# Regrouping the attention scores through HBM and mixing the heads on four 64x64 tiles

## The reference

```python
h = tok_mixer(x)                                  # AFT-like token mixer, layernorm
q, k, v = split(layernorm(h) @ w_qkv)             # 16 heads of 64
attn = softmax(q @ k.T * 64**-0.5, axis=-1)       # (16, 257, 257)
attn = einsum('bhij,hg->bgij', attn, reattn_w)    # mixing of the heads
attn = (attn - mean over heads) * rsqrt(var over heads + 1e-3)
attn = attn * gamma[head] + beta[head]
h = h + (attn @ v) @ w_out + b_out
h = h + down(silu(gate(q8(ln(h)))) * up(q8(ln(h))))   # quantised feed-forward, inner width 1024
```

## Time and profile before

| | |
|---|---|
| median of three runs | 876.7 us |
| profiled execution, its own time | 874.84 us |
| span in the profile | 873.1 us |
| granted TensorE clock, mean | 0.935 |
| loop iterations, from transpose L498 to the next | 93.4 to 96.4 us |

### The profile page before, as it was taken

One profiled execution on the slowest core, in us unless ns is written; L12 is line 12 of the kernel. 1 busy time (PEld: TensorE's weight loads), 2 busy tenths in 40 slices (PEclk: granted clock), 3 DMA queues, 4 the chain that ended last, 5 costly groups with the idle time before them and its releaser, 6 DMA issues.

```text
span 873.1 us, 14228 instructions
## 1 busy us (share of the span) xinstructions
PE 732.1 (84%) x4514; PEld 527.8 (60%) x4514; DVE 642.9 (74%) x1442; ACT 435.2 (50%) x1198; POOL 179.6 (21%) x367
## 2 busy tenths in 40 slices
PE   1769688989998999898998999899998899788754
PEld 0446466757675777666775767477766677456521
DVE  1596758688958896888768885889688886868444
ACT  0103637563657364745747265836575574747210
POOL 0308124012310233013301231023301330013000
PEclk9959799989999999989998999899999999899877
DMA  8300410050003200230004000311023000500000
GB/s 330 129 1 0 172 46 2 17 175 9 31 1 129 72 30 0 85 107 12 24 28 164 6 30 0 128 64 36 0 73 119 13 1 28 166 7 7 1 12 0
DMA packets 25414, 49.26 MB, mean 56 GB/s; under 512 B 2715, under 2 KB 6052, under 8 KB 24740
## 3 DMA queue, kind: packets, MB, share of 16 engines
q1 hardware_dynamic: 24340, 45.34, 15.4%
q10 hardware_dynamic: 1040, 3.49, 1.0%
HBM read 13.16 MB, written 2.11 MB: 17 GB/s over the span
## 4 chain that ended last, share of the span: by engine, by line
PE 37%; issue 26%; DVE 16%; ACT 8%; POOL 8%; DMA 4%; POOLq 1%; SPq 0%; ACTq 0%; DVEq 0%
PE small L535 5%; PE big L535 5%; PE small L686 5%; PE big L552 5%; DMA pg<-pst 4%; PE big L618 4%; DVE pst L1186 3%; DVE mx L1193 2%; ACT pst L918 2%; PE big L716 2%; PE small L641 2%; PE small L671 2%; ACT ot L1007 2%; DVE var L1221 1%; POOL nww L1569 1%
## 5 line engine op out<-in xcount | busy, mean ns | idle before, releaser
L918 ACT ACTIVATE pst<-big,nb 128x256 f32<-128x256 f32 x256 | 117.7, 473 | 46.9 <-DVE nb L1196 24.5
L618 PEld LDWEIGHTS big<-w_mix,pg 128*128 128x128 f32 x1024 | 122.5, 194 | 25.9 <-DVE an L1265 18.3
L618 PE MATMUL big<-w_mix,pg 128*128 128x128 f32 x1024 | 126.3, 279 | 7.9 <-DVE an L1265 7.9
L1193 DVE TENSOR_REDUCE mx<-big 128x4 f32<-128x1024 f32 x64 | 78.2, 1222 | 26.2 <-PE big L552 25.7
L552 PE MATMUL big<-qk_t 64*128 64x256 f32 x512 | 72.6, 402 | 20.1 <-ACT qk_t L901 20.1
L939 ACT ACTIVATE sqb<-big 128x1024 f32<-128x1024 f32 x64 | 64.8, 1014 | 42.9 <-PE big L618 42.9
L1221 DVE TENSOR_REDUCE var<-sqb 128x64 f32<-128x1024 f32 x64 | 77.6, 1213 | 9.1 <-ACT sqb L939 9.1
L1265 DVE TENSOR_TENSOR an<-big,rstd 128x1024 f32<-128x1024 f32 x64 | 78.4, 1225 | 2.7 <-DVE rstd L1252 0.2
L1186 DVE TENSOR_SCALAR pst<-pst,rr 128x256 f32<-128x256 f32 x256 | 72.8, 350 | 0.0
L552 PEld LDWEIGHTS big<-qk_t 64*128 64x128 f32 x512 | 44.2, 186 | 45.6 <-ACT qk_t L901 27.9
L535 PE MATMUL small<-xnt,w_qkv 128*128 128x256 f32 x256 | 65.5, 400 | 0.0
(11 more groups left out here) (200 smaller groups left out, 1233.5 us busy)
## 6 DMA issues: line engine op xcount, KB each, us to landing
pg<-pst SPq DMA_DIRECT2D x128, 256.0 KB
w_qkv<-in_w_qkv SPq DMA_DIRECT2D x1, 3072.0 KB
xt<-in_x_t SPq DMA_DIRECT2D x8, 256.0 KB, 2.9
xr<-in_x_tok SPq DMA_DIRECT2D x8, 256.0 KB, 2.7
out<-h SPq DMA_DIRECT2D x16, 128.0 KB
an<-in_gate_t ACTq DMA_DIRECT2D x1, 1024.0 KB, 8.5
an<-in_up_t ACTq DMA_DIRECT2D x1, 1024.0 KB, 10.8
an<-in_down_t ACTq DMA_DIRECT2D x1, 1024.0 KB, 13.3
```

The source lines that it names most:

```text
L618: last = mm(mix_place(n)[:, i * P:(i + 1) * P], pg[:, hf * (IB // 2) + i, it * T + jt * P:it * T + (jt + 1) * P], w_mix[:], start=True, st ...
L918: last = A(pst[:, g % 2, h % GH, it, :], big[p % 2][:, (j * TT + it) * T:(j * TT + it + 1) * T], ACT.Exp, bias=nb[:, h, it:it + 1], scale= ...
L1193: V.reduce_max(mx[:, hs, :], big[p % 2][:, :].rearrange("p (h t l) -> p h t l", h=2, t=TT), AX)\
```

## The change

The exponentials are no longer normalised. The row sums are written behind the exponentials of a head (columns 512 and 513 of a `pst` row of 520), and each head goes by one DMA into a scratch tensor `turned` in HBM, indexed (k, head, ib, 514 floats), as soon as the sums of its pair are there. When all 16 writes have landed, two DMAs read all of it into `pg`, one for each half of the blocks `ib`, each over all 128 partitions; a partition is now k * 16 + head. DVE takes the reciprocals of the gathered sums (`row_scales`, two instructions of 128x16), and POOL multiplies the constant mixing weights by them (`scale_weights`, four instructions of 128x512, into the free first slot of `pst`). The mixing uses these weights as the moving operand, in 64x64 tiles: 30 matmuls instead of 8 in a group. The class column, its exponential and the sum are now made for each pair, not for each two pairs. The order of tokens is now made by multiplying with a permutation matrix instead of the identity where `xn` and `pck` are turned (so as matmuls, not transposes), and the copies that permuted are plain.

```diff
-    return n // 4, n // 2 % 2, n % 2
+    return n // 4, n % 2, n // 2 % 2
...
-        pst = sb("pst", [P, 2, GH, TT, T])
+        pst = sb("pst", [P, 2, GH, PW])
+        w_rows = pst[:, 0, :, :].rearrange("p j m -> p (j m)")[:, 0:TT * IB * QH * H]\
+            .rearrange("p (t i x) -> p t i x", t=TT, i=IB)
...
+        turned = nc.dram_tensor("turned", (QG, H, IB, SUM + TT), F32, kind="Internal").ap()
...
+                if not is_(b, 0):
+                    for hf in range(2):
+                        sp.wait_ge(s_pg[hf], 16 * b)
+                for p in pairs:
+                    sp.wait_ge(dve_s.sem, dve_s.at(b, ("tot", p)))
+                    for h in (2 * p, 2 * p + 1):
+                        sp.dma_start(turned[:, h, :, :], pst[:, h // GH % 2, h % GH, 0:SUM + TT])\
+                            .then_inc(s_sh[p // 2 % 2][p % 2], 16)
+
+            def gather(b):
+                if is_(b, 0):
+                    sp.wait_ge(setup_pe.sem, setup_pe.at(0, "z"))
+                else:
+                    sp.wait_ge(pe_r.sem, pe_r.at(b - 1, ("r", NMIX - 1)))
+                for s in s_sh[0] + s_sh[1]:
+                    sp.wait_ge(s, 16 * 2 * (NGRP // 2) * (b + 1))
+                for hf in range(2):
+                    ibs = slice(hf * (IB // 2), (hf + 1) * (IB // 2))
+                    sp.dma_start(pg[:, ibs, 0:SUM + TT], turned[:, :, ibs, :].rearrange("q h i m -> (q h) i m"))\
+                        .then_inc(s_pg[hf], 16)
...
-                        last = nc.tensor.transpose(bank[2][:, c * T + tt * P:c * T + (tt + 1) * P],
-                                                   xn[:, tt, c * P:(c + 1) * P], ident[:])
+                        last = mm(bank[2][:, c * T + tt * P:c * T + (tt + 1) * P],
+                                  xn[:, tt, c * P:(c + 1) * P], to_place[:], start=True, stop=True)
...
+                if jt == 0:
+                    if it == 0:
+                        pe.wait_ge(s_pg[hf], 16 * (b + 1))
+                    pe.wait_ge(pool_w.sem, pool_w.at(b, (it, hf)))
                 for i in range(IB // 2):
-                    last = mm(mix_place(n)[:, i * P:(i + 1) * P],
-                              pg[:, hf * (IB // 2) + i, it * T + jt * P:it * T + (jt + 1) * P], w_mix[:],
-                              start=True, stop=True)
+                    ib = hf * (IB // 2) + i
+
+                    for half in ((0, P),) if i == 0 else ((0, 64), (64, P)):
+                        j = slice(it * T + jt * P + half[0], it * T + jt * P + half[1])
+                        for k_hi in range(2):
+                            rows = slice(k_hi * 64, k_hi * 64 + 64)
+                            last = mm(mix_place(n)[half[0]:half[1], k_hi * 512 + i * 64:k_hi * 512 + (i + 1) * 64],
+                                      pg[rows, ib, j], w_rows[rows, it, ib, :], start=True, stop=True)
...
-                A(permuted(xnt[:].rearrange("p c l -> p (c l)")),
-                  bank[2][:, :].rearrange("p (t i k) -> p t i k", i=IB, k=QG), ACT.Copy).then_inc(act_a.sem, 1)
+                A(xnt[:], bank[2][:, :].rearrange("p (c l) -> p c l", c=MC), ACT.Copy).then_inc(act_a.sem, 1)
...
-                    normalise(g, 0)
...
+            def row_scales(b, hf):
+                dve.wait_ge(s_pg[hf], 16 * (b + 1))
+                if not is_(b, 0):
+                    dve.wait_ge(pool_w.sem, pool_w.at(b - 1, (TT - 1, hf)))
+                ibs = slice(hf * (IB // 2), (hf + 1) * (IB // 2))
+                V.reciprocal(rg[:, :, ibs], pg[:, ibs, SUM:SUM + TT].rearrange("p i t -> p t i")).then_inc(dve_w.sem, 1)
...
-                ffn_x(b, ff, P, 1, (dve_o.sem, dve_o.at(b, ("h3", 1))), lambda: ffn_out(b, ff, P, 0))
+                ffn_stats(b, ff, P, 1, (dve_o.sem, dve_o.at(b, ("h3", 1))))
+                if do_scores:
+                    row_scales(b + 1, 0)
+                ffn_norm(b, ff, P, 1)
+                ffn_quant(b, ff, P, 1)
+                ffn_out(b, ff, P, 0)
+                if do_scores:
+                    row_scales(b + 1, 1)
...
+            def scale_weights(b):
+                for hf in range(2):
+                    pool.wait_ge(dve_w.sem, dve_w.at(b, hf))
+                    for it in range(TT):
+                        ibs = slice(hf * (IB // 2), (hf + 1) * (IB // 2))
+                        G.tensor_tensor(w_rows[:, it, ibs, :], w_mix[:].unsqueeze(1).to_broadcast([P, IB // 2, QH * H]),
+                                        rg[:, it, ibs].unsqueeze(2).to_broadcast([P, IB // 2, QH * H]), ALU.mult)\
+                            .then_inc(pool_w.sem, 1)
...
                 power(b, ff["pool"], ff["dve"], ve_f, rs_f, P, slice(1, 2), ("ve", 1))
+                if do_scores:
+                    scale_weights(b + 1)
```

More of the change, by code:

```diff
@@ L77, in group, with place_of @@
 def group(n):
-    return n // 4, n // 2 % 2, n % 2
[L82 to L90, removed]
+    return n // 4, n % 2, n // 2 % 2
+def place_of(token):
+    half, k_hi, i, k_lo = token // 64, token // 32 % 2, token // QH % (IB // 2), token % QH
+    return k_hi * 64 + k_lo * IB + half * (IB // 2) + i
 class Stage:
@@ L264, in build @@
         s_xr = sem("s_xr")
+        s_pg = [sem(f"s_pg{hf}") for hf in range(2)]
         s_sh = [[sem(f"s_sh{slot}{part}") for part in range(2)] for slot in range(2)]
@@ L414, in iteration @@
                     regroup(b + 1)
+                    gather(b + 1)
                 store(b)
@@ L430, in _ @@
             regroup(0)
+            gather(0)
             load(2)
@@ L573, in turn_class @@
                 for it in range(TT):
-                    last = nc.tensor.transpose(bank[2][0:H, it * P:(it + 1) * P], pck[:, it, :], ident[:])
+                    last = mm(bank[2][0:H, it * P:(it + 1) * P], pck[:, it, :], to_token[:], start=True, stop=True)
                 last.then_inc(pe_s.sem, 1)
@@ L917, in scores @@
                             h = 2 * p + j
-                            last = A(pst[:, g % 2, h % GH, it, :],
+                            last = A(pst[:, g % 2, h % GH, it * T:(it + 1) * T],
                                      big[p % 2][:, (j * TT + it) * T:(j * TT + it + 1) * T], ACT.Exp,
@@ L921, in scores @@
                     last.then_inc(act_s.sem, 1)
[L922 to L925, removed]
+                    act.wait_ge(dve_s.sem, dve_s.at(b, ("d", p)))
+                    hs = slice(2 * p, 2 * p + 2)
+                    A(eck[:, hs, :], dck[:, hs, :], ACT.Exp).then_inc(act_s.sem, 1)
                 act.wait_ge(dve_s.sem, dve_s.at(b, "nq"))
@@ L1197, in scores @@
                                            op0=ALU.mult, op1=ALU.min).then_inc(dve_s.sem, 1)
[L1198 to L1205, removed]
+                    dve.wait_ge(dve_s.sem, dve_s.at(b, ("nb", p)))
+                    V.tensor_tensor(dck[:, hs, :], nb[:, hs, :], nsck[:, hs, :], ALU.subtract)\
+                        .then_inc(dve_s.sem, 1)
+                    if p:
+                        total(p - 1)
+                    if p and p % 2 == 0:
                         finish_group(p // 2 - 1)
@@ L1208, in scores @@
                         between[p]()
+                total(HP - 1)
                 finish_group(NGRP - 1)
-                normalise(NGRP - 1, 1)
                 dve.wait_ge(act_s.sem, act_s.at(b, "eq"))
@@ L1492, in _ @@
             mixer_y(1)
+            row_scales(0, 0)
+            row_scales(0, 1)
             mixer_out(1)
@@ L1651, in _ @@
             mixer_values(1)
+            scale_weights(0)
             mixer_out(1)
@@ L1697 @@
         "w_qkv": chunks(x["L0_attn_w_qkv"]).reshape(P, MC, 3 * INNER),
-        "mix_rep": x["L0_attn_reattn_w"][[head_of(r) for r in range(P)]], "mix16": x["L0_attn_reattn_w"],
+        "mix_rep": x["L0_attn_reattn_w"][[r % H for r in range(P)]], "mix16": x["L0_attn_reattn_w"],
         "gamma": np.repeat(x["L0_attn_ln_gamma"], DH).reshape(HP, P).T,
```

55 lines of the change are left out of this document (30 added, 25 removed).

## The result

The kernel after takes 900.59 us (median of 4 runs, 897.12 to 901.61), the kernel before 876.6 us beside it: a ratio of 1.0262, 95% interval 1.0229 to 1.0294, +24 us. The forecast was 883.5 us, +7.0. The profiled execution took 899.8 us, its span is 898.0 us (before 873.1 us), TensorE's mean granted clock 0.907 (before 0.935).

A forecast was written before the change was run, and what follows sets the result against it. TensorE was taken as the bound (85.9 of 94.5 us an iteration, DVE 75.3). Terms -8.0 + 1.8 + 9.1 + 0 + 1.1 + 3.0 = +7.0 gave 881.8 us profiled, 883.7 as median; forecast 883.5, 8-in-10 range 860 to 918.

The forecast's parts named there:

- Normalisation gone: Score phase: removing 9.1 us an iteration of DVE work gains 0, because PE's 3.0 us a pair bounds it.
- Slots free sooner: End of score phase: ACT's wait for DMAs emptying pst slots goes; 1.0 us a phase, -8.0 us over eight phases.
- DMAs: Scratch writes at 196 GB/s and gathers at 350 to 400 GB/s stay hidden in the loop; no cost there.
- the cover of 5 us: Predicted slack between the second gather's landing and DVE's need for it in the loop.
- row_scales: DVE's reciprocals of the sums: first hidden in a wait, second in DVE's serial stretch, 7 x 0.25 = +1.8 us.
- scale_weights: POOL's weight products beside DVE's norm: one norm instruction waits out one 1.27 us product, +9.1 us over 7 iterations.
- The mixing on tiles: Mixing groups of 60 small records take 2.05 us against 1.95 us before, counted as 0 us.
- two rows of before that bounded it: Spacings in the earlier profile giving 3.9 us a mixing group, or 1.2 us with half the columns and twice the tiles.
- my first rival: Mixing: four tiles really run at once, a group takes 1.2 us, -20 us, 863 us; chance 0.25.
- Turns and setup: Extra matmul records turning pck, +1.1 us; setup's row_scales waiting for the gather and POOL's products delaying the norm, +3.0 us.
- The prediction's own marks: Signs of being wrong: groups under 1.5 or over 2.6 us, loop gather wait, clock below 0.93, iteration under 92 us.

The follow-up runs named there:

- the pair with two and four matmuls a block: Kernel after, loops unrolled, first reciprocal moved behind norm and quantisation: four matmuls a block 869.34 us, two of 64x128 921.03 us.
- Written out, the kernel after: Kernel after with the five hardware loops of the engines unrolled, no branch back, same instructions otherwise: 879.56 us, ratio 1.0041 to the kernel before.
- the kernel before written out: Kernel before with its five hardware loops unrolled: 875.90 us, ratio 1.0010 to the kernel before.
- the same 928 us: Kernel after with 42 VectorE setup memsets and five of eight blocks in two matmuls: 928.64 us; also with one setup matmul repeated 27 times: 927.66 us.

## Why the prediction was wrong

The direction was right, the size not: +24 for +7.0. By its steps:

- *Normalisation gone: 0.* Held, as far as shown: the waits of the exponentials that remain are for DVE's `nb` (31.9 us), which waits for PE's scores.
- *Slots free sooner: 1.0 us a phase.* Held: in the intervals of the loop the last exponentials end 41.2 to 41.4 us after the turn, 42.4 to 42.8 us before. No wait of ACT for these DMAs remains.
- *DMAs.* The gather moved 394 GB/s, where I had 350 to 400. But it was issued at 494.76, 49.5 us after the turn, where I had 46 to 47: the writes landed 7.9 us behind the last total of 486.87, not 5. The second gather landed at 507.92 and the second reciprocal began at 510.12: of the cover of 5 us 2.2 were left. DMA windows of the writes' end and the gather:

```profile
484.00:493.00 9.00, 7.93 (x53) 4.57 (x54) 4.51 (x13) 6.00 (x18) 1.40 (x2) 0.81 0.53 186
497.00:504.00 7.00, 7.00 (x33) 5.90 (x32) 5.48 (x5) 0.55 (x1) 0.00 (x0) 1.00 1.04 394
```

- *row_scales: +1.8.* Held, no wait for the gather and 0.24 us in the loop. Outside it they wait, 2.5 and 5.3 us in the setup, 2.4 and 1.6 us behind the last score phase.
- *scale_weights: +9.1.* The mechanism held, on one instruction of the norm and to the end of a product, but a product takes 1.04 us, not 1.27, and the norm lost 0.7 us, not 1.3: +5.
- *The mixing on tiles: 0.* Mis-sized. A group of 60 records takes 1.41 us, not 2.05 (against two rows of before that bounded it, 1.2 was the nearer), and by the pair with two and four matmuls a block that is worth 1.8 us an interval, some -13, where I had taken 0. It is my first rival in a small dose, without its end at 863 us. The price is against two matmuls a block, whose group takes 2.00 us, not against the kernel before with its 1.95; that the tiles gain as much there is not shown.
- *Turns and setup: +1.1 and +3.0.* The setup was too small: interval 1 is 3.2 us longer and the first turn comes 2.2 us later, 5.4 together, 1.8 of them because `mixer_out(0)` ran at half clock (3.78 us for 1.99). The turns were not measured apart.
- *The term that was not there.* The sum had none for the branch back. I counted the 176 matmuls more in eight groups (356 records and as many weight loads) only as PE's time, and 42 instructions fewer in VectorE's setup as nothing at all. This is the step that failed: the runs put 21.0 of the 24 us there. Written out, the kernel after stands at +3.7 beside the kernel before written out; my sum said +7.0. The prediction's own marks, groups under 1.5 us and a clock under 0.93, both showed (1.41 us, 0.907).
- *The rest.* That +3.7 is near +7.0 is partly luck. With -8.0, +1.7 and +5, the tiles' -13, my +1.1 and the setup's 5.4 the sum would be -8, so some 12 us of the written-out kernel are not accounted for. Part may be clock: between the first turn and the last TensorE is at half for 95.3 us there and for 81.7 us in the kernel before written out. What that costs was not measured.

Of the 5.0 us that an interval with a branch is longer than the seventh, `an` comes 2.3 us later; the other 2.7 us are the half clock, 10.2 us of it in place of 3.4. Of half clock at the start of group 3 the runs show: with a stall or a pause it was there in each interval; without one in none to five of six intervals of a kernel. What decides it in two neighbours that run the same instructions stays open.

## What to carry to other kernels

Before a loop gets more instructions on an engine, count them, and read in the profile of before whether instruction packets stop after the first iteration: if they do, the loop stays with the engine, and a change of its length or of its place can cost a stall at every branch back, which the timeline shows only as "issue". When "issue" ends a wait right behind a branch, look at the branch's own record on every engine, as two equal stalls hide each other. A time alone did not tell the experiments apart; the same 928 us stood for two different causes.

## What was not expected of the hardware

- Nine packets of 16 KB (q8, gone when TensorE's loop stays) and five of 8 KB (q14, gone when VectorE's does) per iteration. A branch back then holds TensorE for 3.4 to 3.9 us and VectorE for 2.8 to 3.1 us, and otherwise for 0.2 to 0.3 us. The Trainium skill (Runtime: NRT & Kernel Launch, Instruction fetch mechanics) has blocks of 16 KiB for all engines; the packets of q14 are 8 KB (36 packets, 0.29 MB), and the measurement decides.
- A loop of about 1,640 instructions on TensorE stayed in one place and not in another; 1,450 stayed in the one place tried.
- 60 matmul records of 64x64 take 1.41 us, 0.019 us each, where 32 of 64x128 take 2.00.
- TensorE was granted 1.2 GHz for 20.5 us after 10 us in which it was busy for 9.1 us at 2.4 GHz, and in the neighbouring interval, after 9.2 us, it was not.
